# Vision-transformer tower on one core: the next image's scores ahead of the weighted sums, fp32 row-tiled outputs, and a shorter end

## The reference

```
h = tokens(x)                                   # 16 images x 256 tokens x 192, three patch levels, Hilbert order
h = h + attention(layernorm(h))                 # 12 heads of 16, causal, per image, then W_proj
# feed-forward: a binary tree of router rows
logits = layernorm(h) @ weights_in.T            # 21 nodes
idx = 0
for level in range(10):
    l = logits[idx];  coeff[idx at this level] += gelu(l)
    idx = clip(2*idx + 1 + (l > 0), 0, 20)      # from the fifth level on a token stays in the last node
h = h + coeff @ weights_out                     # 21 x 192
```

## Time and profile before

| | us |
|---|---|
| median of 3 runs | 331.52 (331.21 to 337.34) |
| profiled execution | 332.06 |
| its span, first to last instruction | 330.3 |
| PE busy | 267.7 |
| DVE busy | 224.9 |
| ACT busy | 193.8 |
| POOL busy | 186.3 |
| mean granted TensorE clock | 0.946 |

### The profile page before, as it was taken

The page is one execution under the profiler, slowest core; times in us unless marked ns, Lnnn a source line. Parts: engine busy times, 40 slices in busy tenths (PEclk is TensorE's granted clock), DMA queues, the critical chain, the costliest instruction groups (busy, mean ns, idle before and its releaser), DMA issues.

```text
span 330.3 us, 7883 instructions
## 1 busy us (share of the span) xinstructions
PE 267.7 (81%) x2638; PEld 207.2 (63%) x2638; DVE 224.9 (68%) x1126; ACT 193.8 (59%) x393; POOL 186.3 (56%) x322
## 2 busy tenths in 40 slices
PE   0469061187897989999999999999999999999873
PEld 0446051176776667767767767767767777776662
DVE  1054110055488779889888888898898897967872
ACT  2651022045445867867767767768767656858770
POOL 4727777400203567667676676576676575555662
PEclk9997658579999999999999999999999999999997
DMA  4712311001660824625625625624525423000038
GB/s 110 229 35 43 79 22 18 15 0 54 128 108 14 132 78 88 127 89 78 130 78 84 130 79 84 133 75 80 133 83 79 122 85 83 2 5 2 1 98 285
DMA packets 26720, 27.27 MB, mean 83 GB/s; under 512 B 6834, under 2 KB 26416, under 8 KB 26680
## 3 DMA queue, kind: packets, MB, share of 16 engines
q1 hardware_dynamic: 23176, 23.69, 31.7%
q0 software_dynamic: 1568, 2.36, 3.0%
q10 hardware_dynamic: 1936, 0.72, 0.8%
HBM read 4.34 MB, written 3.15 MB: 23 GB/s over the span
## 4 chain that ended last, share of the span: by engine, by line
PE 59%; DVE 10%; POOL 9%; ACT 6%; DMA 6%; issue 6%; SPq 3%; DVEq 0%; ACTq 0%; POOLq 0%
POOL G L342 9%; PE bank L1342 7%; PE bank L1364 7%; PE bank L1308 6%; PE bank L1257 4%; ACT PT L563 4%; PE bank L1279 3%; PE bank L1284 3%; PE bank L1367 3%; DMA G<-x,I 3%; SPq L295 2%; PE bank L1238 2%; PE bank L1304 2%; PE bank L1346 2%; DVE C L846 2%
## 5 line engine op out<-in xcount | busy, mean ns | idle before, releaser
L846 DVE CUSTOM_DVE_ANT_0 C<-bank,MASKV 128x256 bf16<-128x256 f32 (+1 forms) x384 | 112.8, 350 | 19.9 <-PE bank L1308 15.2
L563 ACT ACTIVATE PT<-bank 128x512 f32<-128x512 f32 x144 | 80.8, 598 | 35.0 <-PE bank L1342 30.5
L363 POOL TENSOR_SCALAR_AFFINE_SELECT PT<-PT 128x256 f32<-128x256 f32 x144 | 68.8, 485 | 52.6 <-ACT PT L563 48.6
L347 POOL TENSOR_TENSOR PART<-RES,PART 128x256 bf16<-128x256 f32 (+1 forms) x31 | 28.1, 906 | 25.7 <-ACT PART L557 25.7
L342 POOL DMA_INDIRECT G<-x,I x32 | 30.3, 948 | 15.3 <-issue 9.5
L802 DVE BATCH_NORM_STATS2 ST<-HT 128x6 f32<-128x192 f32 x32 | 9.5, 348 | 32.9 <-ACT HT L515 32.9
L846 DVE DVE_READ_ACCUMULATOR2_ANT MX<- 128x1 f32 x384 | 31.8, 83 | 0.1
L1342 PE MATMUL bank<-QS,KS 98*128 98x256 bf16 x144 | 27.9, 275 | 3.7 <-ACT PT L563 2.6
L1364 PE MATMUL bank<-PT,VA 128*32 128x256 f32 x384 | 30.5, 386 | 0.0
L1308 PE MATMUL bank<-KS,QS 96*128 96x256 bf16 x144 | 27.6, 273 | 1.4 <-DVE MX L846 1.0
L1159 PE MATMUL bank<-ID,G 128*48 128x128 f32 x32 | 6.7, 362 | 23.1 <-DMA G<-x,I 23.1
(11 more groups left out here) (165 smaller groups left out, 649.4 us busy)
## 6 DMA issues: line engine op xcount, KB each, us to landing
QS<-PART SPq DMA_DIRECT2D x72, 96.0 KB, 3.6
KS<-PART SPq DMA_DIRECT2D x72, 96.0 KB, 3.6
out<-HT SPq DMA_DIRECT2D x7, 384.0 KB, 3.6
KSL<-PART SPq DMA_DIRECT2D x24, 96.0 KB, 3.4
QSL<-PART SPq DMA_DIRECT2D x24, 96.0 KB, 3.6
G<-x,I POOLq DMA_INDIRECT x42, 2.5
out<-HT SPq DMA_DIRECT2D x2, 192.0 KB, 3.7
WFS<-wft ACTq DMA_DIRECT2D x2, 144.0 KB, 3.3
```

The costliest lines, as they stand in the source:

```text
L347: pool.tensor_tensor(parts(b)[2][:, ROUNDS[w], :], RES[:, ROUNDS[w], :], parts(b)[1][:, ROUNDS[w], :], ALU.subtract).then_inc(p2_ok, 1)
L363: pool.affine_select(out=e, in_=e, compare_op=ALU.is_ge, fill=0.0, base=0, pattern=[[0, n], [1, P]], channel_multiplier=-1).then_inc(cut_o ...
L563: nc.scalar.activation(PT[:, v, :], BANK[T_BANK[(SU * par + v) % 2]][:, :], ACT.Exp, scale=SCALE).then_inc(exp_ok, 1)
L846: ins = nc.vector.tensor_tensor_reduce(JUNK[:, n:n + keys], bank[:, j * keys:(j + 1) * keys], MASKV[:, S - keys:S], 1.0, LOWEST, ALU.add, ...
```

## The change

- **Next scores sooner.** In PE's `step(b)` the wait for image b+1's stacks and `scores(b+1, ., 0)` stand behind `project_rest` and ahead of `weighted(d, ., 0)`; in the closing steps the same for image 15. On DVE `row_max(b+1, ., 0)` stands between the two transposes. POOL's second `low` stands ahead of `normalise`. `scores(b, 4)` and `scores_t(d, 3)` are swapped.
- **Fold and centre in the opening.** `centre` (the router's weights with their mean taken out, `WIC`) moves from step 14 to the opening; a new `fold` multiplies it with the projection and puts it beside it in `WP`. SP loads `WEX` and `WPT` behind the constants.
- **Router in the last projection.** Image 15's projection is 192+32 wide: its last 32 columns are the attention's share of the logits, added to logits made from the tokens without it (`own_residual`).
- **Four score banks at the end.** `scores_t` of image 15 uses banks 3, 2, 0, 1 in turn.
- **Newton roots.** The inverse deviations of images 0 to 11 come from POOL (18 small operations, `roots`, in step 14) in place of ACT's square root.
- **Tree in place.** The walk writes both signs straight into `RE` and multiplies them there; rows A and B, and C's walk, on POOL.
- **fp32 row-tiled outputs.** No bf16 terms. Coefficients of four tiles are transposed at once (32 columns each) and multiplied in four row groups of PE; half of the banks have the tokens added by an identity matmul and are copied by ACT, half are added by DVE. Four rounds in place of eight.

```diff
 # SP
+            sp.dma_start(WEX[:, :], wext).then_inc(ld_tree, 16)
+            sp.dma_start(WPT[:, :, :], wpt.rearrange("(c p) n -> p c n", c=2)).then_inc(ld_tree, 16)
...
-            for k in range(NQ - 1):
-                sp.wait_ge(*added(k))
...
+            for k in range(ROUNDS_OUT - 1):
+                sp.wait_ge(od_ok, 2 * (k + 1))
+                sp.wait_ge(oa_ok, 2 * (k + 1))
...
+            for n in range(2):
+                for j, done in ((n, od_ok), (2 + n, oa_ok)):
+                    sp.wait_ge(done, 2 * (ROUNDS_OUT - 1) + n + 1)
+                    sp.dma_start(last_rows[j], HT[:, NB + j:NT:QD, :]).then_inc(out_ok, 16)
 # POOL, step
                 biased(b)
+                if f.off < B:
+                    low(f, 1)
                 if not b.first:
                     normalise(b - 1)
-                if f.off < B:
-                    low(f, 1)
+                if b.first:
+                    pool.memset(CO[:, :, :], 0.0).then_inc(tree_init, 1)
+                if b.late:
+                    roots()
...
             for n in range(B):
                 step(Image(0, n))
...
+            walk(ROWS_A)
             for g in range(G):
                 causal(Image(0, B - 1), g, 0)
                 causal(Image(0, B - 1), g, 1)
 # DVE, step
-                row_max(b, par, 0)
+                if b.off == 1:
+                    row_max(b, par, 0)
...
                 heads_by_token(d, False)
+                row_max(b + 1, 1 - par, 0)
                 heads_by_token(d, True)
 # DVE, end
+            def own_residual():
+                dve.wait_ge(pj_ps, B)
+                dve.wait_ge(hb_ok, B)
+                dve.wait_ge(x2t_ps, B)
+                rows = BANK[MA][:, 0:2 * (D + NP)].rearrange("p (t d) -> p t d", t=TT)
+                nc.vector.tensor_tensor(LG[:, OWN, :], rows[:, :, D:], LG[:, OWN, :], ALU.add).then_inc(ls_ok, 1)
+                hv = HT[:, OWN, :]
+                nc.vector.tensor_tensor(hv, rows[:, :, 0:D], hv, ALU.add).then_inc(h2_ok, 1)
...
+            heads_by_token(last, False)
+            own_heads(True)
+            heads_by_token(last, True)
+            own_heads(False)
+            copy_logits(5)
+            dve.wait_ge(tw_ok, 2)
+            last_node(ROWS_A)
+            copy_logits(6)
+            copy_logits(7)
+            dve.wait_ge(lgd_ok, 4)
+            coefficients_t(0)
+            residual_statistics(before)
+            own_residual()
+            residual_statistics(last)
+            dve.wait_ge(mv2_ok, 2 * B)
+            variances(ROWS_C)
+            dve.wait_ge(pw_ok, 2)
+            visits(ROWS_B)
+            products(2, ROWS_B)
+            last_node(ROWS_B)
+            own_rstd(ROWS_C)
+            dve.wait_ge(ls_ok, 1)
+            scaled(ROWS_C)
+            output(0)
 # PE
+            def stack_in(b, par):
+
+                for w in range(2):
+                    pe.wait_ge(stacked[w][par], 6 * 16 * (b.off // 2 + 1))
+
             def step(b, par):
                 f, d = b + 2, b - 1
                 has_front, has_ahead = f.off < B, f.off + 1 < B
-                for w in range(2):
-                    pe.wait_ge(stacked[w][par], 6 * 16 * (b.off // 2 + 1))
-                scores(b, par, 0)
+                if b.off == 1:
+                    stack_in(b, par)
+                    scores(b, par, 0)
...
                 scores(b, par, 3)
                 scores_t(d, 1 - par, 2)
+                scores(b, par, 4)
                 scores_t(d, 1 - par, 3)
-                scores(b, par, 4)
...
                 if b.off >= 2:
-                    project_rest(b - 2)
+                    project_rest(D)
+                stack_in(b + 1, 1 - par)
+                scores(b + 1, 1 - par, 0)
                 weighted(d, 1 - par, 0)
                 weighted(d, 1 - par, 1)
                 max_t(b)
...
             def closing_step(b, par):
...
+                project(b - 2)
+                if b.late:
+                    stack_in(b + 1, 1 - par)
+                    scores(b + 1, 1 - par, 0)
                 weighted(d, 1 - par, 0)
                 weighted(d, 1 - par, 1)
                 max_t(b)
+                weighted(d, 1 - par, 2)
                 logits(q + 1)
-                weighted(d, 1 - par, 2)
                 logits_back(q + 1)
...
+            def fold():
+                pe.wait_ge(wic_ok, 1)
+                pe.wait_ge(ld_tree, 16 * N_TREE)
+                for c in range(2):
+                    for n in range(3):
+                        ins = nc.tensor.matmul(BANK[O_BANK[0]][:, (2 + n) * NP:(3 + n) * NP], WPT[:, c, n * P:(n + 1) * P], WIC[:, c, :],
+                                               start=c == 0 and n == 0, stop=c == 1, skip_group_check=True)
+                ins.then_inc(wpf_ps, 1)
...
+            logits(5)
+            tokens_t(15)
+            logits_back(5)
             tokens_t(14)
             logits(6)
+            logits(7)
+            pe.wait_ge(ont_ok, B)
+            pe.wait_ge(ot_ok, 2 * B)
+            project_wide(D + NP)
             logits_back(6)
+            pe.wait_ge(ont_ok, B + 1)
+            project_rest(D + NP)
+            logits_back(7)
...
+            def output(k):
...
+                for h in range(2):
+                    for j in range(QD):
+                        ins = nc.tensor.matmul(BANK[OUT_BANK[k][j]][:, h * D:(h + 1) * D], CF[NP * j:NP * j + NODES, k, h, :], WEX[NP * j:NP * j + NODES, :],
+                                               start=h == 0 and j < 2, stop=h == 1 or j > 1, skip_group_check=True)
+                ins.then_inc(o_ps, 1)
```

More of the change, by code:

```diff
@@ L463, in _ @@
+            products(1, ROWS_A)
+            pool.wait_ge(ls_ok, 1)
+            walk(ROWS_C)
         @block.scalar
@@ L1351, in weighted @@
                 pe.wait_ge(cut_ok, b.count(SU, 3 * g + 3))
-                if g == 0 and not b.first:
-                    pe.wait_ge(ot_ok, (b - 1).count(2, 1))
+                if g == 0:
+                    pe.wait_ge(*((wpf_ok, 1) if b.first else (ot_ok, (b - 1).count(2, 1))))
+                    if b.last:
+                        pe.wait_ge(*copied(10))
                 if g == 2:
@@ L1466, in closing_step @@
                 d, q = b - 1, 2 * (b.off - B + 2)
-                for w in range(2):
-                    pe.wait_ge(stacked[w][par], 6 * 16 * (b.off // 2 + 1))
-                scores(b, par, 0)
                 scores(b, par, 1)
+                tokens_t(2 * q)
+                tokens_t(2 * q + 1)
                 scores_t(d, 1 - par, 0)
-                tokens_t(2 * q)
-                if b.late:
-                    centre()
                 scores(b, par, 2)
@@ L1651, in _ @@
+            pe.wait_ge(tree_init, 1)
+            tokens_in(0)
+            pe.wait_ge(lgd_ok, 3)
+            pe.wait_ge(co_ok, 1)
             coefficients_t(0)
-            logits(7)
             coefficients_t(1)
-            logits_back(7)
-            pe.wait_ge(w6_ok, 4 + PARTS)
             output(0)
-            for k in range(2, NQ):
-                coefficients_t(k)
-                output(k - 1)
-            output(NQ - 1)
+            tokens_in(1)
+            output(1)
+            pe.wait_ge(co_ok, 2)
```

571 lines of the change are left out of this document (262 added, 309 removed).

## The result

The changed kernel takes 371.94 us (median of 4 runs, 369.43 to 374.49), the kernel before beside it 331.37. The ratio is 1.1228, with a 95% interval of 1.11 to 1.1357: slower by 12%, against 363 us forecast. It lies 0.94 us above the range of 355 to 371. The profiled run took 374.25 us, its span is 372.5. Executions of one kernel fall at two levels, 331.1 to 331.5 and 337.3 us for the kernel before, 369.4 to 369.6 and 374.3 to 374.5 us for the changed one, so that lower against lower the ratio is 1.116 and the changed kernel takes 369.5 us. The way from the first maxima issue to the end leaves the opening out: it is 263.4 us in the profiled run, and 225.3 in that of the kernel before.

A forecast was written before the change was run, and what follows sets the result against it. TensorE, busy to 96% in the steps, was held to start each step when its stacks land. Span 330.3 + 33.3 (loop and closing steps) - 2.2 (tail) = 361.4, so 363 us; range 355 to 371.

The forecast's parts named there:

- The loop: Steps: stacks land, scores, two weighted sums, max_t, maxima issue, stacks two images on; 14.85 us a step against 12.47.
- the closing steps: Last two steps: image 15's stacks land at 310.35, first ends at 314.1, second at 325.4 in place of 292.08.
- the tail: After the closing steps: 36.0 us in place of 38.2, first output at about 24.3; bounds -7 and +2.
- M to L: SyncE's queue, from an image's maxima issue to the last stack landing two images on: 12.35 us.
- landing to scores: From the last stack landing to the start of the next image's first scores on TensorE: 0.1 us.
- scores to maxima: From the first scores through two weighted sums and max_t to the maxima issue: 0.25 + 2.15 us.
- the 0.7 us gap in the queue: SyncE's wait for GpSimd's second `low`: the change removes it, 0.7 us in the issue, less to the landing.
- Rival 3, the clock: Each TensorE stall halves its clock, so the loop is 16.45 us: +19, 382 us in all; chance 0.05.
- L to M: From the last landing of the next image's stacks to this image's maxima issue: 0.1 + 0.25 + 2.15 us.
- at granted clock 1.00: Sign in the profile: from image 1's maxima to image 13's about 178 us, with TensorE's clock at full level.
- The stretch I set against it: Old kernel, 52 to 56 us: TensorE idle for 4 us yet at clock 1.00, cited against the clock falling.
- Opening: Work ahead of the steps: added matmuls and moved DMAs lie under the gathers; 0, at most +0.5 us.

The follow-up runs named there:

- The move alone in the old kernel: The kernel before with only the wait for the next image's stacks and its first scores moved ahead of the weighted sums: 386.03 and 396.83 us.
- the fillers: The changed kernel with five filler matmuls on TensorE ahead of each moved wait for the stacks: 365.03 us, ratio 1.1032.
- the scores back: The changed kernel with the stacks' wait and first scores at the step's start again: 336.89 us; with the root instructions also spread between GpSimd's masks, 331.59.
- the scores sooner: Scores as changed, SyncE's six first-part stack DMAs ahead of the maxima's: 387.69 us; with roots spread and three tail moves too, 377.43.
- the order mended: The changed kernel with two ScalarE moves in the tail, last logits copy ahead of the gelu, first output evictions ahead of the square root: 368.53 us.
- everything mended and the scores back: The changed kernel with scores at the step's start, roots spread, ScalarE's two tail moves and VectorE's first output eviction earlier: 325.47 us, ratio 0.9784.
- the new stack order: The changed kernel with ScalarE issuing the maxima's DMA and the stack DMAs ordered first parts first: 345.23 us, ratio 1.0417.

## Why the prediction was right, and where it was short

The loop was forecast rightly, in mechanism and nearly in size. Two terms of the sum failed: the closing steps, 4.2 us short, where the 18 root instructions were held to be off TensorE's path, and the tail, 4.7 us short, where ScalarE's work was counted without its order. The clock, put at nothing, is the third. The range was also added up wrongly: its own bounds, 363 + 5.4 + 4, give 372.4 and not 371.

*What bounds the kernel; the loop.* Right. The owner of TensorE's small idle rest became the owner of the whole loss. The loop's terms, forecast and measured: M to L 12.35 and 11.95 (11.6 to 12.6); landing to scores 0.1 and 0.09; scores to maxima 2.4 and 2.35 where the clock held. The first one is 0.4 too long: I reasoned that removing the 0.7 us gap in the queue would bring nothing to the landing, "the transfers, not the issues, set the pace". The move alone in the old kernel kept the gap, 1.3 us there, and had 12.8 to 13.8, so the gap counts. By the Trainium skill ("DMA: Bandwidth & Descriptors", section on the anatomy of one DMA), which fits its price to DMAs that GpSimd issues, the last one would have been down 2.2 us behind its issue, as estimated before; 3.1 to 4.8 us in the changed kernel speak against it again. These DMAs are SyncE's, so the prediction stretched the price.

*Rival 3, the clock.* I gave it 0.05 as an all-or-nothing case and left it out of the forecast. Seven of fourteen turns, five of the twelve steps among them, lost 0.4 to 1.5 us to it, which makes L to M 2.73 in the mean of the twelve for the 2.5 of the forecast and the 2.44 of the undisturbed turns. The sign "at granted clock 1.00" failed: it is 0.96. The loop in sum is 14.68 for 14.85, twelve of them 176.1 for 178.2. The stretch I set against it, idle with the clock at 1.00, decided nothing. Nor does the stall's length alone: the two shortest waits (1.04 and 1.16 us) lost none, but a wait of 1.92 us (image 10) lost 1.5 and one of 2.88 us (image 7) none. The Trainium skill ("TensorE: Matmul & The Clock Gate", section "HAM oscillation") describes groups of matmuls that alternate with waits on DMAs and run slow after each wait. The trace agrees in half of the turns, and so does the profiled execution with the fillers, where no turn was slow.

*Closing steps.* Short by 4.2 us, in two parts. The first ends 5.46 us behind L(15) for 3.75, the clock again (0.59 from 312 to 316, `weighted` 1.08 for 0.64). The second takes 13.79 for 11.3. The step that failed is "the root table loads of ROWS_AB go for 18 POOL operations in step 14, off PE's path". They are on it: GpSimd, end of the block, masks, parts of the maxima, then TensorE behind them.

```profile
324.53 0.23 POOL L393 TENSOR_TENSOR RSTD<-RSTD,SD 128x24 f32<-128x24 f32 x1
324.71 3.96 POOL L352 TENSOR_SCALAR_AFFINE_SELECT PT<-PT 128x256 f32<-128x256 f32 x9
328.63 0.20 POOL L360 CAST MP<-MX 128x24 bf16<-128x24 f32 x1
...
329.21 0.28 PE L1328 MATMUL bank<-IDB,MP 128*24 128x128 bf16 x2 [0.90 <-POOL MP L362]
```

Eighteen linked instructions took 5.5 us (319.25 to 324.7, some 0.3 each), of which I had costed none. The wait of 0.90 us at L1328 is their end. Spread out, they cost 0.65 us less in the step with the scores back (12.26 for 12.91), and 1.34 less with the scores sooner (12.26 for 13.60), which is the changed kernel's case. Of the other 1.15 us, TensorE waits 0.38 and 0.45 at the step's end for ScalarE's two copies around `logits_back`; the rest, 0.3, I can't divide.

*Tail.* Short by 4.7 us: 40.7 for 36.0. The first store goes 27.2 us in, not 24.3, and from it to the end it is 13.6 us for 11.7. I counted ScalarE's work "at its pace" and not in its order, with `logits_t(7)` behind a gelu that waits for GpSimd's scaling and behind a table load. TensorE stood still, and the clock fell (0.64 and 0.51 in the two windows from 356). With the order mended the tail came out at 36.35 with the first store at 24.3, which is the forecast's sum. That it agrees so well is in part luck: the clock still fell in it, which the forecast left out, and in the kernel with everything mended and the scores back, counted the same way, the tail is 34.9 us and the first store 22.5 in. What was left out is a queue's order; the durations were near enough.

*Opening.* 0 to +0.5 forecast, 4.0 in the profiled run (M(0) 109.08 for 105.05). This is not the change's. The kernel with the new stack order has the same instructions on TensorE in the opening, and M(0) at 104.34. TensorE in that kernel, then in the changed one, same matmuls:

```profile
15.05 1.95 PE L1176 MATMUL bank<-G2T,W2S 96*64 96x256 f32 x16 [0.67 <-ACT G2T L488]
19.39 1.99 PE L1140 MATMUL bank<-ID,G 128*96 128x128 f32 x16
```

```profile
14.86 3.68 PE L1183 MATMUL bank<-G2T,W2S 96*64 96x256 f32 x16 [0.67 <-ACT G2T L497]
22.43 3.65 PE L1147 MATMUL bank<-ID,G 128*96 128x128 f32 x16
```

In some executions TensorE's matmuls take nearly twice as long until about 26 us, and the first gather of the last set goes at 26.35 us, not at 21.65 (GpSimd waits for L1147's transposes). The column of the granted clock does not show it, it reads 1.00 there in the changed kernel; that this is the lower level is read from the durations alone. M(0) lies at 104.2 to 106.5 us in six profiles and at 108.9 to 111.9 in seven, whatever the kernel, and in all thirteen the sixteen matmuls shown first take 1.95 us in the six and 3.68 in the seven. The runs of the kernel before show two values as well, about 331.5 and 337.5; its one profile is of the shorter opening.

*The sum.* M(13) comes 2.3 us over the forecast (opening and image 1 +4.4, loops -2.1), the way to L(15) -0.2, the closing steps +4.2, the tail +4.7: 11 us over the span of 361.4. The medians show 9 of them. Some 4 of the 11 are the opening's in this execution. The two shorter executions, 369.4 and 369.6 us, lie within the range; that they are the ones with the shorter opening is not shown, for they have no profile.

*The sign and the chances.* 0.94 for slower was right. The range failed at its upper end. Its terms could go wrong independently (clock, closing steps, tail, opening), and I had summed bounds for the loop and the tail alone, and these to 371 where they give 372.4. Of the bounds the loop kept its own, and the tail did not: its 40.7 us lie above the 40 that I gave it. Opening, closing steps and tail came to 4 to 5 us each, all of one sign. The closing steps and the tail are costs that a count by durations leaves out: an engine's order, and the clock.

## What to carry to other kernels

Before moving a wait forward on an in-order engine, follow what stands behind it all the way round to whoever feeds the awaited buffer. If the path comes back, the wait's length is paid in every turn, and no share of busy time shows it. Put the moved work behind the instruction that feeds the loop, not ahead: here that place was worth 2.2 us a step. The old place, at the start of the step, was better still, by 0.37.

A gap measured in one schedule isn't there in another if the gap was the stall. Ask of each "there is room here" which wait makes the room.

Walk each engine's order with the waits of its neighbours in it before you count a tail by durations. Without them the count was 4.7 us short here; with two moves on one engine 4.4 of them came back.

## What the runs showed of the hardware

- TensorE lost its upper clock level behind seven of fourteen waits in the changed kernel and paid 0.4 to 1.5 us for it each time. The seven were 1.92 to 2.93 us long, the others 1.04 to 2.88. Five matmuls of 192 columns ahead of the wait kept the level in fourteen of fourteen in one execution; two others of the same kernel ran at a lower mean clock (0.937 and 0.934 for 0.951).
- SyncE issues the stack DMAs of a burst 0.64 us apart in the median (0.59 to 0.75). Twelve take 7.6 us, an estimate from that, of one step's 12.2. The last of them landed 2.8 to 5.1 us behind its issue.
- A DMA issued by ScalarE keeps it from its next instruction: between its copy of the maxima and the copy to PART behind it ScalarE stood idle for 0.69 us, where the changed kernel has no gap.
- Linked small operations of GpSimd (128 x 24 elements, each waiting for the one before) stand 0.3 us apart, whichever they are: 0.21 to 0.25 of work and 0.07 of issue.
- The same instructions' opening has two lengths about 5 us apart: the same sixteen matmuls took 1.95 us in six profiles and 3.68 in seven.
